# A bidirectional 1x1-convolution scan: the input add before each store moved from VectorE to GpSimd

## The reference

```python
def step(prev, x_i):
    y = jnp.einsum('oc,nch->noh', Wc, prev) + conv_b[None, :, None]
    y = jnp.where(y >= 0, y, prelu_a * y)
    cur = y + x_i
    return (cur, cur)
x = jnp.moveaxis(feature, 3, 0)
_, fwd_rest = jax.lax.scan(step, x[0], x[1:])
fl = jnp.concatenate([x[0:1], fwd_rest], axis=0)
_, bwd_rest = jax.lax.scan(step, fl[-1], fl[:-1], reverse=True)
out = jnp.concatenate([bwd_rest, fl[-1:]], axis=0)
...
x = x + _L0_conv_ref(_gn(x), L0_conv_conv_w, L0_conv_conv_b, L0_conv_prelu_a)
```

## Time and profile before

| | |
|---|---|
| median of 3 runs | 389.98 us (389.96 to 390.05) |
| the profiled execution, its own time | 390.33 us |
| its span, first to last instruction | 388.6 us |
| mean granted TensorE clock | 0.996 |
| VectorE busy | 295.7 us (76%), 963 instructions |
| GpSimd busy | 5.1 us (1%), 11 instructions |
| ScalarE busy | 224.3 us (58%), 799 instructions |

### The profile page before, as it was taken

One profiled execution on the slowest core, in us unless ns is written; L12 is line 12 of the kernel. 1 busy time (PEld: TensorE's weight loads), 2 busy tenths in 40 slices (PEclk: granted clock), 3 DMA queues, 4 the chain that ended last, 5 costly groups with the idle time before them and its releaser, 6 DMA issues.

```text
span 388.6 us, 10101 instructions
## 1 busy us (share of the span) xinstructions
PE 352.3 (91%) x3080; PEld 351.0 (90%) x3080; DVE 295.7 (76%) x963; ACT 224.3 (58%) x799; POOL 5.1 (1%) x11
## 2 busy tenths in 40 slices
PE   0117799999999999999999999999999999999994
PEld 0117799999999999999999999999999999999994
DVE  2899599999765666566566788878888888888785
ACT  2663066566466566556656655665665566556554
POOL 1011100000000000000000000000000000000000
PEclk9999899999999999999999999999999999999999
DMA  7997000000000000000000112222221222222222
GB/s 248 428 422 307 2 0 1 0 0 1 0 0 0 0 0 0 0 0 0 0 0 0 56 54 81 81 69 66 81 81 55 80 81 72 63 81 81 59 76 82
DMA packets 28231, 26.30 MB, mean 68 GB/s; under 512 B 1344, under 2 KB 25920, under 8 KB 26816
## 3 DMA queue, kind: packets, MB, share of 16 engines
q1 hardware_dynamic: 27936, 26.22, 19.9%
q10 hardware_dynamic: 288, 0.00, 0.0%
HBM read 13.63 MB, written 12.58 MB: 67 GB/s over the span
## 4 chain that ended last, share of the span: by engine, by line
PE 73%; DVE 14%; DMA 6%; issue 4%; SPq 1%; ACT 1%; POOLq 0%; POOL 0%; DVEq 0%
PE psum L196 73%; DVE state L284 6%; DMA xio<-in_x 6%; DVE state L328 4%; DVE state L323 2%; DVE bstat L254 1%; SPq L158 1%; ACT above L237 0%; POOLq L41 0%; POOL rstd L387 0%; DVE xio L340 0%; ACT below L239 0%; DVE chan L264 0%; DVEq L105 0%; DVE var_eps L281 0%
## 5 line engine op out<-in xcount | busy, mean ns | idle before, releaser
L196 PE MATMUL psum<-state,w_t 128*128 (+1 forms) x3008 | 339.3, 276 | 2.8 <-DVE state L284 2.4
L196 PEld LDWEIGHTS psum<-state,w_t 128*128 128x128 f32 x3008 | 338.5, 193 | 3.4 <-DVE state L284 2.5
L237 ACT ACTIVATE above<-psum,bias 128x128 f32<-128x128 f32 x376 | 139.9, 372 | 144.4 <-PE psum L196 144.4
L323 DVE TENSOR_TENSOR state<-above,state 128x128 f32 (+1 forms) x376 | 107.5, 288 | 68.5 <-ACT above L237 66.8
L239 ACT ACTIVATE below<-psum,neg_bias 128x128 f32<-128x128 f32 x376 | 140.2, 373 | 0.0
L328 DVE SCALAR_TENSOR_TENSOR state<-below,neg_slope,state 128x128 f32 (+1 forms) x376 | 123.4, 349 | 6.7
L340 DVE TENSOR_TENSOR xio<-xio,state (+1 forms) x48 | 33.2, 692 | 1.7
L284 DVE TENSOR_SCALAR state<-xio,mean,rstd 128x352 f32<-128x352 f32 (+3 forms) x84 | 30.9, 434 | 1.2 <-POOL rstd L387 1.2
L254 DVE BATCH_NORM_STATS2 bstat<-xio 128x6 f32<-128x512 f32 (+2 forms) x45 | 23.6, 584 | 8.5 <-DMA xio<-in_x 8.4
L176 PE MATMUL psum<-chan,same_group 128*128 128x4 f32 x8 | 2.0, 322 | 25.1 <-DVE chan L264 25.1
L176 PEld LDWEIGHTS psum<-chan,same_group 128*128 128x128 f32 x8 | 1.8, 280 | 25.3 <-issue 14.7
(11 more groups left out here) (17 smaller groups left out, 8.3 us busy)
## 6 DMA issues: line engine op xcount, KB each, us to landing
out_y<-xio SPq DMA_DIRECT2D x48, 256.0 KB, 2.6
xio<-in_x SPq DMA_DIRECT2D x11, 1024.0 KB, 16.2
w_t<-in_w SPq DMA_DIRECT2D x4, 256.0 KB, 19.2
xio<-in_x SPq DMA_DIRECT2D x1, 512.0 KB, 26.4
xio<-in_x SPq DMA_DIRECT2D x2, 256.0 KB, 23.5
bias<-in_bias ACTq DMA_DIRECT2D x1, 2.0 KB, 5.1
slope<-in_slope ACTq DMA_DIRECT2D x1, 0.5 KB, 8.6
```

What stands on the lines that cost most here:

```text
L196: mm = nc.tensor.matmul(psum[:, 4 * par + o, 0:COLS], w_t[:, k, o * P:(o + 1) * P], xs[k], start=k == 0, stop=k == 3)
L237: nc.scalar.activation(above[:, par, o, :], z, ACT.Relu, bias=bias[:, o:o + 1], scale=1.0).then_inc(above_done, 1)
L323: nc.vector.tensor_tensor(sts[o], above[:, par, o, :], sts[o], ALU.add).then_inc(part_done, 1)
```

## The change

`add_input` moves from the VectorE block to the GpSimd block, with the same wait (the fourth `state_ready` of its step), the same operands and the same `out_ready` behind it. On VectorE it stood inside a loop of two steps per turn. On GpSimd it is written out 48 times with constant addresses, behind the four powers. VectorE's backward loop is left with the eight operations of `slot(False)`.

```diff
-            def add_input(j, step):
-
-                place = ready(dve, xio_step(dve, step))
-                result = ready(dve, state_step(dve, step))
-                dve.wait_ge(state_ready, reg(dve, j * 4 + 4, 1, 4 * STEPS))
-                return nc.vector.tensor_tensor(place, place, result, ALU.add)
-
...
             loop(dve, beside, FWD, slot(True))
-            add_input(FWD - 1, W - 1).then_inc(out_ready, 1)
-
-            def slot_out(j, par):
-                slot(False)(j, par)
-                add_input(j, target(j, False)).then_inc(out_ready, 1)
-
-            loop(dve, FWD, STEPS, slot_out)
+            loop(dve, FWD, STEPS, slot(False))
...
+            def add_input(j, step):
+
+                place = ready(pool, xio_step(pool, step))
+                result = ready(pool, state_step(pool, step))
+                pool.wait_ge(state_ready, reg(pool, j * 4 + 4, 1, 4 * STEPS))
+                return nc.gpsimd.tensor_tensor(place, place, result, ALU.add)
+
+            add_input(FWD - 1, W - 1).then_inc(out_ready, 1)
+            for j in range(FWD, STEPS):
+                add_input(j, target(j, False)).then_inc(out_ready, 1)
```

## The result

| | before | after |
|---|---|---|
| median, same chip | 390.50 us (20 runs) | 391.31 us (20 runs) |
| ratio, with its 95% interval | | 1.0020 (1.0012 to 1.0028) |
| profiled execution, its own time and its span | 390.33, 388.6 us | 390.56, 388.8 us |
| VectorE busy | 295.7 us | 265.5 us |
| GpSimd busy | 5.1 us | 65.9 us |

The account below looks back on a forecast made before the run. TensorE was taken to bound the kernel. Removed adds 0, held `part` 0 +1.9 and the end +0.65 us gave +2.6 on 389.98, so 392.6 us, with a range of 390.3 to 398.4.

Parts of the forecast that it names:

- What bounds the kernel: Whole scan: TensorE is busy throughout at 3.57 us a step; 47 of VectorE's adds lie in idle time, worth 0.
- The length of the add: GpSimd add of 128x512: 1.08 to 1.38 us, taken as 1.21, starting 0.08 us behind the last `whole`.
- The end: Last `whole` to last store: 1.40 us where 0.75 stood, +0.65 us (+0.52 to +0.82).
- Exclusion: Backward steps: VectorE's `part` 0, with two SBUF inputs, cannot run beside the GpSimd add and starts only when it is over.
- The loop over two steps: Backward steps: a late `part` 0 returns after two steps, so a step takes at least (5.88 + D) / 2.
- D: Time from the last `whole`'s end to `part` 0's start: 1.13 us in backward steps before, forecast 1.35 (1.29 to 1.40).
- VectorE's round: Backward steps: VectorE alone needs D + 2.2 us a step, which sets the step above D of about 1.52.
- the threshold of 1.27: Backward steps: up to D = 1.27 us the 0.13 us of slack hides a late `part` 0; beyond it steps lengthen.
- the 1.9 us for the steps: Backward steps: the held `part` 0 makes TensorE late 46 times by 0.042 us, 1.9 us together.
- the hidden case: Rival for the backward steps: free overlap or a short add leaves only the end, +0.5 to +0.7, 390.6 us; chance 0.30.
- The loss forecast as likeliest: Whole kernel: +2.6 us, from contention between the GpSimd add and `part` 0 plus the longer end; chance 0.50.
- the bound of 0.2%: Whole kernel: a measurement can tell about 0.2%, 0.8 us, from no change; slower than that had chance 0.67.

Follow-up runs that it names:

- runs 2 to 5: Changed kernel with the first 47 GpSimd adds delayed by a memset of 16, 128 or 384 elements, or until the next `above`: 394.19, 395.98, 405.69, 425.90 us.
- runs 2 to 4: Changed kernel with a GpSimd memset of 16, 128 or 384 elements ahead of each of the first 47 adds: 394.19, 395.98, 405.69 us.
- run 5: Changed kernel in which each of the first 47 GpSimd adds also waits for the next step's first `above`, starting beside `part` 0: 425.90 us.
- runs 7 and 8: Changed kernel with five one-element VectorE memsets ahead (391.10 us; with last add on VectorE 390.65), then also 30 on GpSimd (391.56); changed kernel repeated (391.32).
- run 2: Changed kernel with a GpSimd memset of 16 elements ahead of each of the first 47 adds: 394.19 us, ratio 1.0091.

## Why the prediction was wrong

- **What bounds the kernel** held: TensorE does, the adds in the steps were worth nothing, and only the last counts.
- **The length of the add**: 1.21 us taken, 1.265 measured, within 1.08 to 1.38, and 0.1 above the 1.17 that stood beside it as another estimate. The range was carried on from a select of 128 elements, so that it held is partly luck. The start at 0.08 us held.
- **The end**: +0.65 forecast, 1.37 - 0.75 = +0.62 measured. The way back to SyncE took 0.03 us (26 or 27 ns behind each of the 48 adds) and not 0.11, which made up for the longer add.
- **Exclusion** held in kind (runs 2 to 5).
- **The loop over two steps** held. With D as the trace has it (the end of `part` 0, less its usual 0.293, less the end of `whole` 3) it gives 3.627 for D = 1.374 (measured 3.630), 3.674 for 1.468 (3.679), and VectorE's round gives 3.89 for 1.686 (3.883).
- **What failed is the term D.** I put `part` 0's start at the end of the add, 1.35 us behind `whole` 3, so that its whole 0.29 us came after it. The add does end at 1.35 (0.08 + 1.265). But `part` 0 ends 0.15 us behind the add and not 0.29: over 42 steps the held operation ends 0.145 to 0.151 us behind the add in the kernels with the adds as they are, up to 0.153 in those of runs 2 to 4, and 0.148 to 0.154 in run 5. So D counts as 1.35 - 0.145 = 1.20. That is under the threshold of 1.27, which was right, and the 1.9 us for the steps (46 x 0.042) are 0: the steps stay at 3.573 us. The choice among the values was between 1.29 and 1.40, as if the operation that is held had to begin from nothing. No value under the add's end was in my bounds.
- **Why 0.15**: `whole` 0, which takes 0.35 us by itself, ends 0.15 behind the add as well. The two operations have different lengths and the same 128 elements, and VectorE's add of 512 elements (692 ns) against its `part` (293) makes (692 - 293) / 384 = 1.04 ns an element, 0.133 us for 128. It fits that the held operation spends its fixed part, by this about 0.16 us for `part`, while it is held, and only its elements wait. An earlier release, when the add has done its reading, would have to come at different distances (0.145 and 0.20 us) for the two. No run varies the element count of the held operation, so the first is the better fit, and it isn't shown.
- **Not in the sum**: 0.24 us of a late `whole` 1 and 0.29 of a later end, which both go away when code is shifted (runs 7 and 8). The forecast's +2.6 less 1.9 plus 0.5 is 1.2, against 1.1 in the trace and 0.8 in the runs.

So the hidden case came about (390.6 forecast for it, +0.6, 0.30 chance), by exclusion with a smaller D and not by free overlap or a short add. The measured 391.31 lies inside the range of 390.3 to 398.4, but that does nothing for the mechanism: 0.5 us of it is the kernel before, which measured 390.50 beside it and not 389.98, and another 0.5 by the trace are the two terms that no one had forecast. The loss forecast as likeliest was three times the real one, and "slower" is true by the bound of 0.2% only just.

## What to carry to other kernels

Before work moves off an engine, look at whether the bounding engine ever waits for that work. Here TensorE waited for none of the 47 adds in the steps, so taking them off VectorE was worth nothing, and the only add on the path got nearly twice as long by moving (0.69 to 1.26 us). When two engines exclude each other, reckon with the end of the held operation and not with its start. Here that end came 0.15 us behind the holder's, for operations of 0.29 and 0.35 us. The slack decides by hundredths: 0.07 us of holding cost nothing, and 0.18 us more (run 2) made each step 0.057 us longer, 2.6 us in 46 steps.

## What was new about the hardware

- A GpSimd fp32 add of 128x512 takes 1.265 us (1.259 to 1.267 for 48), and VectorE's takes 0.692. SyncE issues a store 0.03 us behind the GpSimd add that it waits for.
- A VectorE operation with two SBUF inputs that is issued while this add runs ends 0.15 us behind it, whether it takes 0.29 or 0.35 us alone. One that is already running is not held, and the add takes 1.31 instead of 1.27 us. A GpSimd memset of 480 elements didn't hold the operation of 0.35 us.
- The place of code goes with tenths in the trace: 0.24 us in VectorE's last step, and a last store that lands in 2.70 to 3.00 us instead of 2.57 when a load of 8192 bytes of code runs beside it. Five one-element instructions on VectorE took the first away, 30 on GpSimd the second. The 0.35 us between GpSimd's closing instructions in the two kernels with the last add on VectorE may be of this kind. No run shows it.
